# A decoder layer in one kernel: fewer idle products, rotation partners by transfers, and sums, scatters and the last statistics in another order

## The chip, the cores and the metric

The kernel runs on one core of a Trainium2 chip. The metric is the device time of one execution in microseconds (us), the median of several runs. Engines are named as the profile names them: PE is TensorE (PEld its weight loads), DVE is VectorE, ACT is ScalarE, POOL is GpSimd, SP is SyncE, which here only issues transfers.

## The reference, cut to what matters

A decoder layer on `x` of 32 sequences of 128 tokens with 128 features, all float32:

```
x = x + self_attention(layernorm(x))     # 16 heads of 8, rotary positions, softmax over 128 keys
x = x + cross_attention(layernorm(x), ctx)   # ctx: 32 x 77 x 128, softmax over 77 keys
h = layernorm(x)
x = x + layernorm(h + experts(h)) * gamma + beta   # the layernorm of the ffn, eps 1e-5
# experts: logits = h @ Wg + bg, the two largest of 8, softmax over these two;
#          y_e = gelu(h @ W1[e] + b1[e]) @ W2[e] + b2[e]  (128 -> 512 -> 128)
# rotary: q*cos + rot(q)*sin, where rot swaps neighbouring features and negates one of each pair
```

The scatter and gather of the experts' rows is the kernel's own way: the reference computes all eight experts.

## The kernel before

The five engines each have a program of their own, and semaphores tie them. Everything of one core is written out by hand as a list of 64 **steps**. A step is one sequence through one attention. The first 12 steps are self attention alone (sequences 0 to 11), then 20 slots give two steps each, self attention of sequence n and cross attention of sequence n - 12, and the last 12 steps (52 to 63) are cross attention alone. Four sequences make a group; there are eight groups. What is done by group (the normalised and transposed input `xnt`, the projections q, rq, k, rk, v, the same for cross attention, the gate's logits, the places of the routed rows) are **items** that `plan()` (L101) hangs into steps; `jobs` are its other entries for DVE, POOL, ACT and SP.

rq and rk are the rotation's partners: products of the input with weights whose neighbouring columns are swapped. DVE multiplies q by cosines and rq by sines (L1368, from PSUM, with the bias), POOL adds the two (`turned`, L1775), ACT and POOL split the sum into two float16 parts (`high`, `low`), SP parks them in DRAM and spreads them from there over the rows that the scores read.

PE's order in one step (`step`, L984): `shifted(st, 0)` (the transposed scores of heads with the maxima taken off, L841 and L847, and between them the plain scores of the step two ahead, L797), `rows_turned` of the step two back (L891), items, idle products (`dense`, L978), `maxima_turned` (L879), `values` of the step before, second half (L873), items, `projected` (L898, L899), `shifted(st, 1)`, `sums_turned` of the step before (L886, which waits for `s_res`, DVE's residual), items, and `values(st, 0)`, which has idle products of its own in front. The **idle products** multiply constants and write to an unused part of a bank. `idle_at` says how many there are: none in a step with projections, three at each of the two places in other steps, six in the last twelve.

DVE's order: maxima of two banks (L1319), items, `residual` (L1346), maxima of two more, `norm_rows` (L1328, L1330, on the turned sums), `residual_statistics`, items. ACT's: two exponentials (L1140), `rows_out`, `sums_out`, `maxima_out`, items, two exponentials, and `high_part`.

After the gate each token's row goes with an indirect DMA to its two experts' regions in DRAM (`scatter`, L1860), from two to each step. As soon as groups 0 to 5 are there (`EARLY` = 5) and DVE has made the table of the first 40 tiles (`first_owners`, `first_sums`, `first_entries`), the expert stage starts: 71 tiles of 128 rows, each transposed (L1080), multiplied (L1069), passed through gelu (L1269), multiplied (L1095), scaled and scattered (L1931). The last attention step, and the last groups' routing, are folded into its first turns (`between`). At the end both rows of each token are added on PE in eight chunks of four sequences (L1121), DVE takes their statistics, POOL the deviations (L1956 to L1960), ACT normalises (L1289), DVE or POOL multiply by gamma (L528) and DVE adds (L1711).

Of the kernel before, what the change touches and what calls it, by code (L numbers as in the profile page):

```python
# [27 lines left out]
P = 128  # L28
SEQS, L, D, LC = 32, 128, 128, 77
H, HD = 16, 8  # L30
GS = 4
# [39 lines left out]
BETA = 3  # L71
NA = ((EARLY + 1) * TOK * TOPK - E * (P - 1)) // P // ROUND * ROUND
# [28 lines left out]
def plan():  # L101
# [14 lines left out]
    for g in range(NG):  # L116
        own = SELF_STEP[g * GS + GS - 1]
        if g >= 2:
            free = SELF_STEP[(g - 2) * GS + GS - 1]
            made = free if g >= 4 else 3 * g - 4 if g == 3 else 1  # L120
            xnt = made - 1 if g >= 4 else made
            if g == 2:
                job(0, "normed", g)
            else:
                job(xnt - 3, "statistics", g)
                job(xnt - 2, "normed", g)
            put(xnt, 1 if g >= 4 else 0, "xnt", g)
            for k, names in enumerate((("q", "rq"), ("k", "rk"))):
                at, turn = (made, 3) if k and g == 3 else (made + k, 1)
                put(at, turn, names[0], g)  # L130
                put(at, turn, names[1], g)
                job(at, "sum", (g, k))
                job(at + 1, "high", (g, k))
                job(at + 2, "low", (g, k))
                job(at + 2, ("park_q", "park_k")[k], g)
            job(made + 2 if g == 3 else made + 3, "spread", g)
            put(free + 3 if g >= 4 else free + 1, 1, "v", g)
# [68 lines left out]
def decoder_layer(nc, x, ctx_t, w_self, b_self, bp, w_cross, b_cross, bo, wg, bg, w1, b1, w2, b2,  # L206
# [3 lines left out]
    with stack:  # L210
# [230 lines left out]
        s_rhi = sem("s_rhi")  # L441
        s_route = sem("s_route")
# [80 lines left out]
        LAST = CHUNKS - 1  # L523

# [72 lines left out]
        def _(sp):  # L597
# [88 lines left out]
            for n in range(NS):  # L686
# [18 lines left out]
                for g in jobs_at(n, "load_x"):  # L705
                    load_x(g)
                if n == 20:
                    for k in range(2):
                        sp.wait_ge(s_st[k], NJ // 2 * (SELF_STEP[(FAR[-1] + 1) * GS - 1] + 1))
# [62 lines left out]
        def _(pe):  # L772
# [211 lines left out]
            def step(st):  # L984
# [114 lines left out]
            def between(i):  # L1099
                if i == -3:  # L1100
                    sums_turned(STEPS[-1])
# [16 lines left out]
            for n in range(CHUNKS):  # L1118
# [6 lines left out]
        def _(act):  # L1125
# [41 lines left out]
            def work(name, g):  # L1167
                bank, c = item(name, g)
                w = BANKS[bank]
                if name in ("q", "rq", "k", "rk", "log", "pos", "cnt"):  # L1170
                    return
                act.wait_ge(s_w[bank], c)
                if name == "xnt":
# [111 lines left out]
            for i in range(SEQS):  # L1285
                if i % FC == 0:
                    act.wait_ge(s_rsfm, i // FC + 1)
                r = SUM[i // FC][:, (i % FC) * D:(i % FC + 1) * D]
                act.activation(xn3all[:, i * D:(i + 1) * D], r, ACT.Identity,  # L1289
# [3 lines left out]
        def _(dve):  # L1293
# [63 lines left out]
            def work(name, g):  # L1357
# [4 lines left out]

# [185 lines left out]
            def step(st):  # L1548
# [33 lines left out]
                if st.at == COUNTED + 2:  # L1582
                    first_sums()
# [101 lines left out]
            def chunk_statistics(n):  # L1685
                dve.wait_ge(s_add, n + 1)
                for i in range(FC):
                    V.bn_stats(stf[:, n * FC + i, :], SUM[n][:, i * D:(i + 1) * D]).then_inc(s_rawf, 1)
# [3 lines left out]
                dve.wait_ge(s_stf, (n + 1) * FC)  # L1692
                V.tensor_scalar(nmf[:, n * FC:(n + 1) * FC], mvf[:, n * FC:(n + 1) * FC, 0], -1.0, None, ALU.mult).then_inc(s_nmean, 1)
# [33 lines left out]
        def _(pool):  # L1727
# [42 lines left out]
            def turned(g, k):  # L1770

                for name in (("q", "rq"), ("k", "rk"))[k]:
                    bank, c = item(name, g)
                    pool.wait_ge(s_wf[bank], c)
# [89 lines left out]
            def scatters(n, place):  # L1864
                for g, i, k in jobs_at(n, ("scatter", place)):
                    pool.wait_ge(s_st[1], NJ // 2 * n + place + 1)
# [9 lines left out]
            def step(st):  # L1876
# [76 lines left out]
            def inverse_deviations(n):  # L1953
                at = slice(n * FC, (n + 1) * FC)
                pool.wait_ge(s_nmean, n + 1)
                G.tensor_scalar(rsf[:, 1, at], mvf[:, at, 1], 4 * EPS, None, ALU.add).then_inc(s_rsf, 1)  # L1956
                pool.wait_ge(s_rsf, 2 * n + 1)
                G.tensor_tensor(rsf[:, 0, at], rsf[:, 1, at], halff[:, at], ALU.pow).then_inc(s_rsf, 1)
                pool.wait_ge(s_rsf, 2 * n + 2)
                G.tensor_tensor(rsf[:, 1, at], nmf[:, at], rsf[:, 0, at], ALU.mult).then_inc(s_rsfm, 1)  # L1960
# [82 lines left out]
```

## Time and profile before

| | |
|---|---|
| median of 3 runs | 603.55 us (601.19 to 603.73) |
| the profiled execution | 598.75 us, its span 596.9 us |
| busy | PE 519.3, DVE 385.3, POOL 347.1, ACT 324.3 us |
| chain that ended last | PE 57%, issue 11%, DVE 9%, DMA 7%, ACT 6%, SP's queue 5%, POOL 4% |
| granted TensorE clock | 0.978 of full on average |

Busy time is the time in which an engine executed an instruction; the chain is followed back from the last instruction to what released each. The ends of matmuls are modelled, so groups that overlap show more busy time than they take in a row.

### The profile page before, as it was taken

The numbers are of one execution on the slowest core, as the hardware profiler recorded it, in microseconds if no ns is written. First come the engines' busy times: TensorE is split into PE (matmuls) and PEld (weight loads), VectorE is DVE, ScalarE is ACT, GpSimd is POOL, SyncE is SP. The second block draws the span as 40 slices with busy tenths as digits, with TensorE's granted clock in tenths as the row PEclk, the third lists the DMA queues.
The fourth block names the chain that finished last, engine by engine and source line by source line (L and its number), as shares of the span: only waits on it lengthen the run. The fifth ranks groups of instructions, "written<-read, shape, count | busy, mean of one in ns | idle before, by whom it ended". The sixth has DMA issues, their size and how long they took to land.

```text
span 596.9 us, 21959 instructions
## 1 busy us (share of the span) xinstructions
PE 519.3 (87%) x7657; PEld 389.0 (65%) x7658; DVE 385.3 (65%) x1275; ACT 324.3 (54%) x870; POOL 347.1 (58%) x475
## 2 busy tenths in 40 slices
PE   6889998989998998888979998789888899999980
PEld 4456565656655655665657676588877799999530
DVE  5778887777886786685855766544644444445096
ACT  2447565766766666665656465445434455555143
POOL 5748597636438748638573467546554554444374
PEclk8999999999999999999999999889999999999995
DMA  5232340431762403403112210022222222222393
GB/s 155 84 115 71 104 152 28 151 91 52 226 230 87 137 20 87 137 25 102 34 40 74 80 47 25 28 55 60 64 68 80 74 69 57 57 57 59 98 252 88
DMA packets 68785, 52.57 MB, mean 88 GB/s; under 512 B 8752, under 2 KB 65077, under 8 KB 68690
## 3 DMA queue, kind: packets, MB, share of 16 engines
q1 hardware_dynamic: 62994, 41.92, 25.1%
q0 software_dynamic: 4352, 8.53, 4.4%
q8 instruction: 59, 0.97, 0.7%
q10 hardware_dynamic: 1344, 0.85, 0.5%
q14 instruction: 36, 0.29, 0.2%
HBM read 33.10 MB, written 18.64 MB: 87 GB/s over the span
## 4 chain that ended last, share of the span: by engine, by line
PE 57%; issue 11%; DVE 9%; DMA 7%; ACT 6%; SPq 5%; POOL 4%; DVEq 0%; ACTq 0%; POOLq 0%
PE S L1069 8%; PE AV L873 7%; PE AV L1095 4%; PE SM L1095 4%; PE ST L841 4%; PE W L921 4%; PE ST L847 4%; PE SM L886 3%; ACT prob L1140 3%; PE AV L978 3%; PE SM L898 2%; DVE nmp L1319 2%; SPq L637 2%; PE W L934 2%; PE SM L891 2%
## 5 line engine op out<-in xcount | busy, mean ns | idle before, releaser
L1140 ACT ACTIVATE prob<-ST 128x512 f32<-128x512 f32 (+1 forms) x256 | 138.4, 592 | 117.3 <-PE ST L847 111.1
L1319 DVE TENSOR_REDUCE nmp<-S 128x4 bf16<-128x308 f32 (+1 forms) x251 | 134.6, 576 | 15.8 <-PE S L797 10.0
L1269 ACT ACTIVATE va<-S,b1s 128x128 f32<-128x128 f32 x284 | 81.1, 369 | 81.0 <-PE S L1069 66.8
L1931 POOL DMA_INDIRECT expert_out<-va,ks x71 | 70.0, 985 | 73.4 <-DVE va L1644 44.7
L1860 POOL DMA_INDIRECT routed<-pay,dest x64 | 65.9, 1029 | 33.3 <-PE ST L847 20.2
L873 PE MATMUL AV<-prob,va 77*32 77x128 f32 (+1 forms) x2048 | 84.4, 280 | 0.6 <-issue 0.5
L1069 PE MATMUL S<-va 128*128 128x128 f32 x568 | 77.7, 280 | 7.6 <-issue 5.5
L841 PE MATMUL ST<-nmt,onesr 32*77 32x128 bf16 (+1 forms) x1024 | 73.7, 219 | 8.9 <-ACT prob L1140 3.3
L1069 PEld LDWEIGHTS S<-va 128*128 128x128 f32 x568 | 70.3, 195 | 10.1 <-issue 8.8
L841 PEld LDWEIGHTS ST<-nmt,onesr 32*77 32x77 bf16 (+1 forms) x1024 | 52.4, 102 | 33.5 <-issue 31.8
L873 PEld LDWEIGHTS AV<-prob,va 77*32 77x32 f32 (+1 forms) x2048 | 49.0, 109 | 24.4 <-issue 20.8
L1828 POOL TENSOR_SCALAR ve<-mv 128x1 f32<-128x1 f32 x64 | 15.7, 245 | 62.2 <-DVE mv L1355 61.7
L886 PE MATMUL SM<-idf,ots 128*128 128x128 f32 x128 | 27.2, 294 | 16.5 <-DVE x L1346 11.3
L1095 PE MATMUL AV<-w2s,va 128*128 x288 | 40.6, 284 | 0.0
L1830 POOL TENSOR_TENSOR rs<-ve,half 128x1 f32<-128x1 f32 x64 | 36.7, 574 | 5.3
L1095 PE MATMUL SM<-w2s,va 128*128 x280 | 39.4, 284 | 0.0
L1644 DVE SCALAR_TENSOR_TENSOR va<-AV,ks 128x128 f32<-128x128 f32 x36 | 12.6, 351 | 40.3 <-remote 15.0
L978 PE MATMUL AV<-onesr,idb 128*128 128x256 bf16 x255 | 38.0, 273 | 0.3 <-ACT x2all L1134 0.3
L847 PE MATMUL ST<-q2s,k2s 32*77 32x128 f16 x512 | 35.8, 214 | 0.0
L1095 PEld LDWEIGHTS AV<-w2s,va 128*128 128x128 f32 x288 | 35.0, 192 | 0.8
L1631 DVE COPY va<-w1s 128x512 f32 x71 | 30.5, 430 | 6.9 <-PE S L1069 5.3
L1095 PEld LDWEIGHTS SM<-w2s,va 128*128 128x128 f32 x280 | 34.0, 192 | 0.7
(278 smaller groups left out, 1133.2 us busy)
## 6 DMA issues: line engine op xcount, KB each, us to landing
ks<-routed SPq DMA_DIRECT2D x72, 65.0 KB
q2s<-q_parts SPq DMA_DIRECT2D x32, 128.0 KB
qs<-q_parts SPq DMA_DIRECT2D x20, 128.0 KB
ks<-k_parts SPq DMA_DIRECT2D x20, 128.0 KB, 2.7
k2s<-k_parts SPq DMA_DIRECT2D x32, 77.0 KB
xin<-x SPq DMA_DIRECT2D x8, 256.0 KB, 3.4
q_parts<-q2part SPq DMA_DIRECT2D x8, 256.0 KB
w1s<-w SPq DMA_DIRECT2D x8, 256.0 KB, 4.4
```

What stands on the lines that cost most here:

```text
L841: mm(o, onesr[rows, b, 0:st.keys], nmt[rows, st.at % 2, :], start=True, stop=False)
L847: ins = mm(o, k, q, start=False, stop=True)
L873: last = mm(AV[32 * c:32 * c + 32, m * L:(m + 1) * L], v[0:st.keys, st.group % 2, at:at + VW], prob[0:st.keys, j, b * L:(b + 1) * L], star ...
L886: last = tr(TURNED[:, m * L:(m + 1) * L], ots[:, m * L:(m + 1) * L], idf[:, :])
L978: mm(bank, idb[:, :], some[:, 0:bank.shape[1]], start=True, stop=True)
L1069: last = mm(S[k][:, q * P:(q + 1) * P], w1c[:, k, q * P:(q + 1) * P], xt[:, (c + 1) % 4, :], start=True, stop=True)
L1095: last = mm(o, ht[:, (c - 1) % 4, q, :], w2s[:, bass.ds(e * (HID // D) + q * D, D)], start=False, stop=(q == HC - 1))
L1140: act.activation(prob[0:st.keys, j, :], ST[j % 2][0:st.keys, :], ACT.Exp, scale=SCALE).then_inc(s_exp, 1)
L1269: last = act.activation(ht[:, (c + 1) % 4, q, :], S[k][:, q * P:(q + 1) * P], ACT.Gelu, bias=b1s[:, bass.ds(b + q, 1)])
L1319: V.tensor_reduce(nmp[:, st.at % 2, row_tile(p), 0:NB], bank[:, 0:NB * st.keys].rearrange("p (b k) -> p b k", b=NB), AX.X, ALU.max, negate ...
L1860: pool.indirect_dma_start(out=routed, out_offset=bass.IndirectOffsetOnAxis(ap=dest[:, g % 2, i, k:k + 1].bitcast(U32), axis=0), in_=pay[:, ...
L1931: pool.indirect_dma_start(out=expert_out, out_offset=bass.IndirectOffsetOnAxis(ap=xr[:, at % ROUND, D + 1:D + 2].bitcast(U32), axis=0), in ...
```

## The change

- For groups 4 to 7 (`SWAP` = 4) rq and rk are not made. ACT moves q (and k) with its bias from PSUM to `rb`; SP copies the odd partitions of `rb` to the even ones of `ra` and the other way round; one step later DVE multiplies `ra` by sines and `rb` by cosines (`rotate`), and POOL adds. All that follows of these groups comes one step later.
- `idle_at`: the second place has none in steps without projections (3 before), and 3 in the last twelve (6 before). The first place keeps its numbers. The first three turns of the expert stage get two idle products of 512 columns each.
- `sums_turned` stands behind `values(st, 0)` instead of in front of it.
- Group 5's eight scatters are in three steps (3, 3, 2) instead of four; the table of the first tiles is made one step earlier.
- In the last stage the first chunk is summed in two halves in two banks, and the negated means are computed by POOL instead of DVE.

```diff
+SWAP = 4
@@ plan()
-                put(at, turn, names[1], g)
+                if g < SWAP:
+                    put(at, turn, names[1], g)
+                else:
+                    job(at, "swap", (g, k))
+                    at += 1
+                    job(at, "rotate", (g, k))
...
-            job(made + 2 if g == 3 else made + 3, "spread", g)
+            job(made + 2 if g == 3 else made + 3 if g < SWAP else made + 4, "spread", g)
...
-                    job(chosen + 1 + i, ("scatter", k), (g, i, k))
+                    n = TOPK * i + k
+                    if g == EARLY:
+                        job(chosen + 1 + n // 3, ("scatter", n % 3), (g, i, k))
+                    else:
+                        job(chosen + 1 + i, ("scatter", k), (g, i, k))
@@ sync
+            def swap(g, k):
+                bank, c = item(("q", "k")[k], g)
+                sp.wait_ge(s_wf[bank], c)
+                sp.wait_ge(s_parts, 2 * (g - 1) + k + 1)
+                sp.dma_start(ra[0::2, k, :], rb[1::2, k, :]).then_inc(s_swap[k], 16)
+                sp.dma_start(ra[1::2, k, :], rb[0::2, k, :]).then_inc(s_swap[k], 16)
@@ tensor
-                return 3 if st.slot < SEQS else 6
+                return (3, 0)[m] if st.slot < SEQS else (6, 3)[m]
...
+                background(st, 2)
+                values(st, 0)
                 if before:
                     sums_turned(before)
-                background(st, 2)
-                values(st, 0)
...
             def between(i):
+                if i < 0:
+                    dense(2, ST[1][:, :])
...
-            for n in range(CHUNKS):
+            for m in range(2):
+                at = slice(m * FC // 2 * D, (m + 1) * FC // 2 * D)
+                for k in range(TOPK):
+                    pe.wait_ge(s_y2[k][0], 16)
+                    last = mm((SUM[0], SUM[LAST])[m][:, at], idf[:, :], y2[0][:, k, at], start=(k == 0), stop=(k == TOPK - 1))
+                last.then_inc(s_add, 1)
+            for n in range(1, CHUNKS):
+                if n == LAST:
+                    pe.wait_ge(s_norm, FC)
@@ scalar
+                if name in ("q", "k"):
+                    k = ("q", "k").index(name)
+                    act.wait_ge(s_sum, 2 * (g - 1) + k + 1)
+                    act.activation(rb[:, k, :], w[:, :], ACT.Identity, bias=bqk[:, 2 * k:2 * k + 1]).then_inc(s_wf[bank], 1)
@@ vector
+            def rotate(g, k):
+                dve.wait_ge(s_swap[k], 32 * (g - SWAP + 1))
+                for part, table in ((ra, sinb), (rb, cosb)):
+                    p3 = part[:, k, :].rearrange("p (i l) -> p i l", i=GS)
+                    V.tensor_tensor(p3, p3, table[:, :].unsqueeze(1).to_broadcast([P, GS, L]), ALU.mult).then_inc(s_rot, 1)
...
                 if st.at == COUNTED + 2:
-                    first_owners()
-                if st.at == COUNTED + 3:
+                    first_sums()
                     first_entries()
...
+                for g, k in jobs_at(st.at, "rotate"):
+                    rotate(g, k)
...
                     take_tiles()
-                if st.at == COUNTED + 2:
-                    first_sums()
+                    first_owners()
...
-                V.tensor_scalar(nmf[:, n * FC:(n + 1) * FC], mvf[:, n * FC:(n + 1) * FC, 0], -1.0, None, ALU.mult).then_inc(s_nmean, 1)
@@ gpsimd
             def turned(g, k):
+                if g >= SWAP:
+                    pool.wait_ge(s_rot, 2 * (2 * (g - SWAP) + k + 1))
...
+                scatters(n, 2)
...
-                pool.wait_ge(s_nmean, n + 1)
+                pool.wait_ge(s_stf, (n + 1) * FC)
                 G.tensor_scalar(rsf[:, 1, at], mvf[:, at, 1], 4 * EPS, None, ALU.add).then_inc(s_rsf, 1)
+                G.tensor_scalar(nmf[:, at], mvf[:, at, 0], -1.0, None, ALU.mult).then_inc(s_nmean, 1)
```

## Rows read from the trace of the kernel before

**Rows 1.** Part 1 of the page: busy us (share of the span), instructions.

```profile
PE 519.3 (87%) x7657; PEld 389.0 (65%) x7658; DVE 385.3 (65%) x1275; ACT 324.3 (54%) x870; POOL 347.1 (58%) x475
```

**Rows 2.** Windows: length, busy PE, PEld, DVE, ACT, POOL, clock, DMA share, GB/s.

```profile
36.00:317.00 281.00, 250.85 (x4897) 168.70 (x4890) 212.27 (x656) 175.28 (x423) 176.85 (x254) 1.00 0.33 99
317.00:383.00 66.00, 60.05 (x1130) 44.35 (x1128) 43.25 (x191) 37.74 (x92) 36.31 (x57) 1.00 0.16 45
383.00:396.00 13.00, 8.98 (x58) 7.12 (x58) 5.38 (x21) 4.97 (x15) 6.82 (x14) 0.63 0.21 51
```

**Rows 3.** Groups by form: operation, shapes, count | busy us, mean ns | idle before, releasers.

```profile
L1319 DVE TENSOR_REDUCE nmp<-S 128x4 bf16<-128x512 f32 x123 | 79.1, 683 | 4.4 <-PE S L797 3.8
...
L1860 POOL DMA_INDIRECT routed<-pay,dest x64 | 65.9, 1029 | 33.3 <-PE ST L847 20.2 <-issue 12.8 <-DVE va L1644 0.3
...
L978 PE MATMUL AV<-onesr,idb 128*128 128x256 bf16 x255 | 38.0, 273 | 0.3 <-ACT x2all L1134 0.3
...
L886 PE MATMUL SM<-idf,ots 128*128 128x128 f32 x128 | 27.2, 294 | 16.5 <-DVE x L1346 11.3 <-DVE x2all L1346 4.8
...
L1368 DVE SCALAR_TENSOR_TENSOR rb<-W,bqk,sinb 128x512 f32<-128x512 f32 x14 | 10.5, 748 | 1.4 <-PE W L921 0.5
...
L1192 ACT ACTIVATE q2part<-W,bqk 128x512 f16<-128x512 f32 x8 | 5.5, 687 | 4.9 <-PE W L943 4.9
...
L1393 DVE TENSOR_TENSOR ra<-ra,rb 128x512 f32<-128x512 f32 x2 | 1.4, 692 | 0.2
```

**Rows 4.** The chain: start, us, what; first and last of 11 such pieces.

```profile
114.65 0.33 PE AV L978 x3
...
377.05 0.66 PE AV L978 x6
```

**Rows 5.** Timeline of step 27, where k of group 6 is made.

```profile
178.02 1.98 PE L921 MATMUL W<-xnt,wqk 128*128 128x512 f32 x4
...
179.84 0.38 PE L898 MATMUL SM<-wcross,onormt 128*128 128x128 f32 x2
...
180.04 0.75 DVE L1368 SCALAR_TENSOR_TENSOR rb<-W,bqk,sinb 128x512 f32<-128x512 f32 x1
...
180.71 0.28 DVE L1346 TENSOR_TENSOR x2all<-SM,x 128x128 f32<-128x128 f32 x1
...
182.66 0.33 PE L891 MATMUL SM<-idf,onorm 128*128 128x128 f32 x1
```

**Rows 6.** The chain at the change-over to the experts.

```profile
370.99 1.03 POOL pay L1841
...
380.16 3.88 DMA routed<-pay,dest
...
385.21 0.86 DMA ks<-routed
```

**Rows 7.** Timeline of the last stage.

```profile
557.90 7.51 PE L978 MATMUL W<-onesr,idb 128*128 128x512 bf16 x34 [0.45 <-DVE va L1644]
...
569.01 0.24 POOL L1956 TENSOR_SCALAR xnt<-xnt 128x4 f32<-128x4 f32 x1 [9.05 <-DVE xnt L1693]
...
569.12 0.89 DVE L1688 BATCH_NORM_STATS2 xnt<-S 128x6 f32<-128x128 f32 x4 [0.20 <-PE S L1121]
...
574.93 1.17 DVE L1693 TENSOR_SCALAR xnt<-xnt 128x4 f32<-128x4 f32 x1
...
576.19 0.70 POOL L1956 TENSOR_SCALAR xnt<-xnt 128x4 f32<-128x4 f32 x1
```

**Rows 8.** Who waited for ACT's copy of the rows: us in total, times.

```profile
  PEld SM L898: 12.7, 24
```

**Rows 9.** Timeline of PE at the change-over.

```profile
380.77 0.41 PE L886 MATMUL SM<-idf,ots 128*128 128x128 f32 x2 [1.45 <-DVE x2all L1346]
...
387.10 0.45 PE L1080 MATMUL W<-idf,ks 128*128 128x128 f32 x1 [2.16 <-DMA ks<-routed]
```

**Rows 10.** A window around the change-over, columns as in rows 2.

```profile
380.00:395.00 15.00, 10.20 (x83) 7.85 (x84) 7.09 (x30) 4.87 (x15) 7.07 (x13) 0.66 0.21 50
```

More of the change, by code:

```diff
@@ L441, in decoder_layer @@
         s_rhi = sem("s_rhi")
+        s_swap = [sem(f"s_swap{k}") for k in range(2)]
+        s_rot = sem("s_rot")
         s_route = sem("s_route")
@@ L523, in decoder_layer, with summed @@
         LAST = CHUNKS - 1
+        def summed(i):
+            bank = SUM[LAST] if FC // 2 <= i < FC else SUM[i // FC]
+            return bank[:, (i % FC) * D:(i % FC + 1) * D]
         def times_gamma(eng, first, seqs, s):
@@ L706, in _ @@
                     load_x(g)
+                for g, k in jobs_at(n, "swap"):
+                    swap(g, k)
                 if n == 20:
@@ L1169, in work @@
                 w = BANKS[bank]
-                if name in ("q", "rq", "k", "rk", "log", "pos", "cnt"):
+                if name in ("rq", "rk", "log", "pos", "cnt") or name in ("q", "k") and g < SWAP:
                     return
                 act.wait_ge(s_w[bank], c)
-                if name == "xnt":
+                if name in ("q", "k"):
+                    k = ("q", "k").index(name)
+                    act.wait_ge(s_sum, 2 * (g - 1) + k + 1)
+                    act.activation(rb[:, k, :], w[:, :], ACT.Identity, bias=bqk[:, 2 * k:2 * k + 1]).then_inc(s_wf[bank], 1)
+                elif name == "xnt":
                     move(turned_of(g)[:, :], w[:, :], s_wf[bank])
@@ L1287, in _ @@
                     act.wait_ge(s_rsfm, i // FC + 1)
-                r = SUM[i // FC][:, (i % FC) * D:(i % FC + 1) * D]
-                act.activation(xn3all[:, i * D:(i + 1) * D], r, ACT.Identity,
+                act.activation(xn3all[:, i * D:(i + 1) * D], summed(i), ACT.Identity,
                                bias=rsf[:, 1, i:i + 1], scale=rsf[:, 0, i:i + 1]).then_inc(s_norm, 1)
@@ L1361, in work @@
                 if name in ("q", "rq", "k", "rk"):
+                    if g >= SWAP:
+                        return
                     n = ("q", "rq", "k", "rk").index(name)
@@ L1685, in chunk_statistics @@
             def chunk_statistics(n):
-                dve.wait_ge(s_add, n + 1)
-                for i in range(FC):
-                    V.bn_stats(stf[:, n * FC + i, :], SUM[n][:, i * D:(i + 1) * D]).then_inc(s_rawf, 1)
+                for i in range(n * FC, (n + 1) * FC):
+                    dve.wait_ge(s_add, n + 2 if n or i >= FC // 2 else 1)
+                    V.bn_stats(stf[:, i, :], summed(i)).then_inc(s_rawf, 1)
                 dve.wait_ge(s_rawf, (n + 1) * FC)
@@ L1691, in chunk_statistics @@
                     V.bn_aggr(mvf[:, i, :], stf[:, i, :]).then_inc(s_stf, 1)
-                dve.wait_ge(s_stf, (n + 1) * FC)
-                V.tensor_scalar(nmf[:, n * FC:(n + 1) * FC], mvf[:, n * FC:(n + 1) * FC, 0], -1.0, None, ALU.mult).then_inc(s_nmean, 1)
             gammas = 0
@@ L1770, in turned @@
             def turned(g, k):
-                for name in (("q", "rq"), ("k", "rk"))[k]:
-                    bank, c = item(name, g)
-                    pool.wait_ge(s_wf[bank], c)
+                if g >= SWAP:
+                    pool.wait_ge(s_rot, 2 * (2 * (g - SWAP) + k + 1))
+                else:
+                    for name in (("q", "rq"), ("k", "rk"))[k]:
+                        bank, c = item(name, g)
+                        pool.wait_ge(s_wf[bank], c)
                 G.tensor_tensor(ra[:, k, :], ra[:, k, :], rb[:, k, :], ALU.add).then_inc(s_sum, 1)
@@ L1865, in scatters @@
                 for g, i, k in jobs_at(n, ("scatter", place)):
-                    pool.wait_ge(s_st[1], NJ // 2 * n + place + 1)
+                    pool.wait_ge(s_st[1], NJ // 2 * n + min(place, 1) + 1)
                     scatter(g, i, k)
@@ L1959, in inverse_deviations @@
                 pool.wait_ge(s_rsf, 2 * n + 2)
+                pool.wait_ge(s_nmean, n + 1)
                 G.tensor_tensor(rsf[:, 1, at], nmf[:, at], rsf[:, 0, at], ALU.mult).then_inc(s_rsfm, 1)
```

## The prediction

> **What bounds the kernel now.** I read the totals of the engines first [rows 1]: TensorE (PE) is busy for 87% of the span, no other engine above 65%. Then the stages [rows 2]. The attention stage, 36 to 383 us, is 347 us long; PE works in 250.85 + 60.05 = 310.9 us of it and stands for 36.1 us. From 383 to 396 us the kernel changes over to the experts, and PE works 8.98 of 13.00 us at a granted clock of 0.63. Then the experts run, and the last 40 us are the sum of the two experts' rows, the last normalisation and the stores. The third view is the groups of instructions [rows 3]: the reader is to see that in the attention stage the largest single cause of PE's standing is DVE's residual (L1346), for which the two transposes of the sums (L886) wait 16.5 us in all. The fourth is the chain of work that ended last [rows 4]: idle products are part of it, but few of them. The last views are the timelines of one step, of the change-over and of the end.
>
> So PE is the bound of attention, with DVE close behind (212.27 us of 281). That matters, since several of the edits take work from PE and none from DVE.
>
> **Rotation partners by transfers.** Groups 4 to 7 lose the projections rq and rk. In the step that makes k of group 6 the two products, k and rk, begin at 178.02 us and the next product (L898) at 179.84 [rows 5]: 1.82 us, 0.91 for one. Eight go: 7.3 us off PE. DVE loses 16 passes from PSUM of 748 ns (12.0 us) [rows 3] and gets 16 multiplications of two SBUF operands; the nearest row is L1393, 128x512 with both operands in SBUF, 692 ns [rows 3]: 11.1 us. DVE's load thus stays, but its place moves: from before the residual of the same step to the end of the next step, behind which the next step's maxima wait. ACT gets eight 128x512 passes from PSUM with a bias; the row of the same form is L1192, 687 ns [rows 3]: 5.5 us, while PE's next product, the projection L898 and the shifts go on, and ACT idles there anyway (it is busy 54% of the span [rows 1]). SP issues 16 transfers of 128 KB. What queues behind them on SP are the parks and spreads of the same and the next step. The transfers have a whole step (5.5 us on average: 347 over 63) before DVE asks for them, and a 65 KB load of rows in this trace is there 0.86 us after its issue [rows 6]. I cost them at nothing; if that cover is gone, DVE stands, and behind it all maxima. POOL's sum and the parts come one step later; group 4's rows are then spread three steps before their first use, about 16 us.
>
> How much of 7.3 us stays? In the step of [rows 5] DVE's residual came at 180.71, 0.87 us after the L898 of 179.84, because DVE had the rb pass (0.75 us from 180.04) in front of it; without that, PE is through this step some 0.9 us earlier. But the moved 1.4 us (two of 692 ns) then stand in front of the maxima of the next step, which in that trace have no slack of this size: a DVE pass of 683 ns per bank [rows 3], two banks before the scores can go on. I walked the pair of steps through: PE comes to the transpose L891 of the step after at nearly the same time as before. Bounds: 0 and 7.3 us gained. I take the middle, 3.5.
>
> The Trainium skill, "SBUF — State Buffer", section "Who interferes with whom", says that a VectorE instruction with two SBUF inputs contends with a GpSimd instruction that reads SBUF, and that the second one to issue blocks. This speaks against the change, whose 16 new multiplications are of this kind where the old ones had one operand in PSUM. The end of the kernel shows it: POOL's 128x4 addition takes 0.24 us in the open and 0.70 us beside a DVE pass of two SBUF operands [rows 7]. If each of the 16 held POOL for its whole 0.69 us, it would be 11 us of POOL, which has some 40% free in this stage; the sum stays as it is.
>
> **Fewer idle products.** With no projection in a step there are three idle products (six in the last twelve) at each of two places. The change takes those of the second call (ahead of the transpose of the maxima, L879) away, and three of six in the last twelve: 20 x 3 + 9 x 3 = 87 products. Three take 0.33 us on the chain, six 0.66 [rows 4]: 87 are 9.6 us of PE. The cover of most of them: the projection L898 behind them waits for ACT's copy of the rows, which comes after two exponentials, and would wait longer without them (PE's weight loads waited for this copy in 24 cases even so, 12.7 us in all) [rows 8]. On the chain I count 11 pieces at this place, from 114.65 to 377.05 us, six of 0.33 and five of 0.66 us; what goes is 6 x 0.33 + 5 x 0.33 = 3.6 us. In steps 60 and 61 POOL sets the pace: the transposes L947 wait for its L1841, which ends at 372.02 [rows 6], and POOL's third scatter in step 60 (about 1.0 us [rows 3]) uses what slack it had. I take 0.6 off: 3.0 us. Bounds 0 and 9.6.
>
> **Sums behind values.** The transposes L886 wait for DVE's residual, 16.5 us in total [rows 3]. Behind `values` (L873, 0.57 us) and its idle products that wait is mostly over. But where does the stall go? In the steps in which the residual is late, DVE is late as a whole: after it come two maxima (up to 1.37 us) and only then the two operations on the turned sums, whose result the transpose L891 waits for. In [rows 5]: residual at 180.71, L891 at 182.66, 1.95 us on, and DVE's two maxima and two operations on the sums take most of it. PE arrives earlier at L891 and stands there instead. Only where the two maxima are short (the 308 columns of a cross step, not 512) does something stay. Where the residual was not late, the sums come 0.6 to 0.9 us later to DVE; there DVE is still in its maxima for most of that, so little is lost. I take 4.0 us gained, bounds 3 lost (0.05 in each of 62 steps) and 16.5 gained.
>
> **Scatters and tables one step earlier.** Group 5's last scatter is issued at 380.16 and lands 3.88 us later, SP's first load of rows comes at 385.21 [rows 6], and PE's first transpose of an expert tile waits 2.16 us until 387.10 [rows 9]. Before that PE stood 1.45 us for a residual that DVE reached late, since the table's entries stood in front of it [rows 9]. The granted clock is 1.00 in the whole stage before [rows 2] and 0.66 on average from 380 to 395 us [rows 10]: with TensorE's two levels, 2.4 and 1.2 GHz, that is 0.34/0.5 of 15 us, 10.2 us, at the lower one, just after the pause for the residual. PE was busy for 10.20 of those 15 us, so for about 6.9 at the lower level, half of it lost: 3.5 us. With eight scatters in three steps the last is issued in step 62, near 374.5 instead of 380.16; the table is done in the same step. The data is then there before PE asks. 2.16 + 1.45 + 3.5 = 7.1 us; the six new idle products of 512 columns cost 0.22 each (7.51 us for 34 [rows 7]), 1.3 us: 5.8 us. Bounds: 0.9 (the data wait alone, less the idle products) and 7.1.
>
> **The end.** The first chunk is summed in two banks by halves, so DVE can start half of four passes (1.8 us) earlier, 0.9 us. It gains nothing: DVE comes to the second chunk at 569.12 after a wait for its sum [rows 7] and will wait for it again. The negative mean moves from DVE (L1693; one of the eight took 1.17 us [rows 7]) to POOL, whose addition at 576.19 starts when DVE's mean is there and is followed by powers and the second gamma pass, for which DVE waits. Chunks 1 to 4 lie ahead of that gamma pass, 0.24 us more each: about 1.0 lost; DVE's shorter end and the earlier start of the last deviations give back 0.4. I take 0.6 lost, bounds 1.5 lost and 1.0 gained.
>
> **Sum.** 3.5 + 3.0 + 4.0 + 5.8 - 0.6 = 15.7 us. The profiled execution took 598.75 us (its span of 596.9 and 1.85 around it); it would take 583.1. The runs shown lie higher (601.19 to 603.73); their median of 603.55 less the same sum is 587.9, rounded to 588.
>
> **Rivals.** (1) DVE, not PE, is what attention has to wait for. For it: the step of [rows 5], and that DVE's work is unchanged. Against: DVE is busy 76% there and PE 89%. Then edits one and three give nothing, and the idle products 2 us: 2 + 5.8 - 0.6 = 7.2 us, 596.4. Chance 0.21. (2) PE alone is the bound, and what DVE does fits in beside it: 7.3 + 6 of the idle products + 12 of the 16.5 + 7.1 - 0.6 = 32 us, 571.5. Chance 0.10. (3) The other side: with 87 fewer products PE's clock falls in attention. The mechanism is that of [rows 10]: a pause, and 10.2 us at the lower level. If PE is busy throughout, one such period costs 5.1 us. Four of them (20.4 us) eat the 15.7 us and put it 4.7 us above before, 608; three (15.3) leave it where it was. For it: PE stands for 36.1 us in attention. Against: none of them brought the clock down between 36 and 380 us (1.00 in both stages of [rows 2]), and the change shortens the pauses as well. Chance 0.07. The Trainium skill, "TensorE: Matmul & The Clock Gate", section "HAM oscillation — how this bites in real kernels", describes such a kernel, which loses its clock again and again behind its waits for data; the trace shows this only at the change-over. (4) The swaps come late behind other transfers and DVE stands 1 to 2 us in each of eight steps: 3.5 turns into -8; the sum is 4.2 us, 599. Chance 0.04.
>
> **From this to the numbers.** My forecast (578 to 595) has 0.58, the four rivals 0.42. Half a per cent, 3 us, is about what can be told from no change here: faster means under 600.5. That holds for the forecast, for rival 2, and for nearly all of rival 1; rival 4 lies near the edge. Faster 0.84, same 0.08, slower 0.08. The range that leaves no more than two in ten outside reaches down to near rival 2 and up over rival 1: 575 to 600.
>
> **What the profile after would show.** L978 on AV 168 times instead of 255; L921 16 instances fewer. PE's wait in front of L886 nearly gone, and a wait in front of L891 on DVE's onorm, some microseconds. DVE's rotations at about 690 ns without a wait for a transfer. The attention stage 10 us shorter. SP's first load of rows right behind step 62 and no PE wait of 2 us behind the last L899; a clock at 1.00 through the change-over. At the end L1693 gone and POOL's part of the chain longer, the last stage no shorter. What would make me wrong: a granted clock below 1.00 inside attention; a gain in attention over 20 us (DVE has more slack than I give it), or under 4 (it has none); the clock still falling at the change-over.

## The result, and the profile after

The changed kernel takes 623.01 us (median of 4 runs, 621.33 to 625.55) against 603.64 us before: 1.033 of the time of before, 95% interval 1.028 to 1.038. It is slower, where I had forecast 588 us. Here and below, medians are over all runs, while ratios and intervals leave out the runs that lie more than 1.5% above the fastest of the same kernel, so a ratio need not be the quotient of two medians.

Part 1 and the clock line of the page of the changed kernel (the second is in 40 slices of the span, in tenths of full speed):

```profile
PE 538.8 (87%) x7564; PEld 397.3 (64%) x7565; DVE 380.8 (61%) x1267; ACT 329.9 (53%) x878; POOL 348.1 (56%) x483
...
PEclk9999798996999898998959886699899999999995
```

Its windows, with the columns of [rows 2]; the third is the place of [rows 10]:

```profile
36.00:317.00 281.00, 251.72 (x4645) 165.93 (x4645) 205.31 (x638) 174.88 (x415) 170.93 (x246) 0.92 0.34 103
317.00:383.00 66.00, 58.48 (x1025) 40.89 (x1019) 36.80 (x149) 33.51 (x83) 30.52 (x51) 0.86 0.19 53
383.00:396.00 13.00, 12.71 (x133) 8.38 (x133) 7.81 (x29) 5.68 (x14) 8.86 (x11) 0.50 0.07 23
```

The clock was 1.00 in the first two of these windows before [rows 2]; now it is 0.92 and 0.86. The trace has eleven periods at the lower level between 36 and 400 us where before had one, at the change-over. The last exponential of attention starts at 402.7 us, not at 379.9: all of the loss is there.

Groups of the changed kernel, with the columns of [rows 3]:

```profile
L1007 PE MATMUL AV<-onesr,idb 128*128 128x256 bf16 x168 | 29.3, 304 | 1.5 <-ACT nmt L1174 1.1 <-ACT x2all L1174 0.3
L915 PE MATMUL SM<-idf,ots 128*128 128x128 f32 x128 | 29.2, 312 | 1.7 <-DVE x L1389 1.4
L920 PE MATMUL SM<-idf,onorm 128*128 128x128 f32 x64 | 22.0, 343 | 5.2 <-DVE onorm L1373 1.6 <-issue 1.4
L950 PE MATMUL W<-xnt,wqk 128*128 128x512 f32 x32 | 17.4, 648 | 1.5 <-ACT xnt L1174 1.5
L1371 DVE RECIPROCAL rden<-SM 128x16 f32<-128x16 f32 x64 | 16.2, 253 | 36.7 <-PE SM L915 35.2 <-issue 1.5
L1437 DVE TENSOR_TENSOR rb<-rb,cosb 128x512 f32<-128x512 f32 x8 | 5.5, 683 | 0.0
L1437 DVE TENSOR_TENSOR ra<-ra,sinb 128x512 f32<-128x512 f32 x8 | 5.3, 661 | 0.0
```

The mechanics are as forecast: 168 idle products, 16 instances fewer of the projection, rotations of 0.66 to 0.68 us without a wait for a transfer, PE's wait ahead of the sums (now L915) down from 16.5 to 1.7 us, and a wait of 5.2 us ahead of the next transpose (L920). One row was not forecast: DVE stands 36.7 us in front of its reciprocal (L1371), waiting for the turned sums. The same row before:

```profile
L1328 DVE RECIPROCAL rden<-SM 128x16 f32<-128x16 f32 x64 | 15.8, 248 | 1.9 <-PE SM L886 1.9
```

The reader is to see in the longer means of PE's rows (304 ns for an idle product, 273 before [rows 3]) that the clock is mixed into every duration.

### The profile page after: what moved, and what is told of

Its sections match the earlier page's. It is cut to its first block, busy times and chain, and to the rows that moved or that the text cites. A ratio compares the mean times of both kernels' runs of the same rounds, so it can differ in the third digit from the quotient of the medians.

```text
span 619.5 us, 21797 instructions
## 1 busy us (share of the span) xinstructions
PE 538.8 (87%) x7564; PEld 397.3 (64%) x7565; DVE 380.8 (61%) x1267; ACT 329.9 (53%) x878; POOL 348.1 (56%) x483
## 4 chain that ended last, share of the span: by engine, by line
PE 55%; DVE 12%; issue 9%; DMA 6%; POOL 6%; ACT 5%; SPq 5%; another core or an unknown queue 1%; DVEq 1%; POOLq 0%; ACTq 0%
PE S L1098 8%; PE AV L902 7%; PE AV L1124 4%; PE ST L870 4%; ACT prob L1180 4%; PE SM L1124 4%; DVE nmp L1362 4%; PE ST L876 4%; PE W L950 3%; PE AV L1007 3%; PE SM L927 3%; SPq L656 2%; PE S L826 2%; PE SM L915 2%; PE SM L920 2%
## 5 line engine op out<-in xcount | busy, mean ns | idle before, releaser
L870 PE MATMUL ST<-nmt,onesr 32*77 32x128 bf16 (+1 forms) x1024 | 82.9, 231 | 17.9 <-ACT prob L1180 10.6
L902 PE MATMUL AV<-prob,va 77*32 77x128 f32 (+1 forms) x2048 | 89.8, 295 | 0.3 <-issue 0.3
L870 PEld LDWEIGHTS ST<-nmt,onesr 32*77 32x77 bf16 (+1 forms) x1024 | 56.8, 109 | 43.9 <-issue 42.3
L902 PEld LDWEIGHTS AV<-prob,va 77*32 77x32 f32 (+1 forms) x2048 | 51.7, 115 | 24.0 <-issue 17.8
L876 PE MATMUL ST<-q2s,k2s 32*77 32x128 f16 x512 | 40.8, 230 | 0.0
L1371 DVE RECIPROCAL rden<-SM 128x16 f32<-128x16 f32 x64 | 16.2, 253 | 36.7 <-PE SM L915 35.2
L826 PE MATMUL S<-k2s,q2s 32*128 32x77 f16 x512 | 32.0, 209 | 1.4 <-DVE nmp L1362 1.4
```

The costliest lines, as they stand in the source:

```text
L826: ins = mm(scored(st, p)[:, b * st.keys:(b + 1) * st.keys], q, k, start=True, stop=True)
L870: mm(o, onesr[rows, b, 0:st.keys], nmt[rows, st.at % 2, :], start=True, stop=False)
L876: ins = mm(o, k, q, start=False, stop=True)
L902: last = mm(AV[32 * c:32 * c + 32, m * L:(m + 1) * L], v[0:st.keys, st.group % 2, at:at + VW], prob[0:st.keys, j, b * L:(b + 1) * L], star ...
```

## The experiments

The experiments ran in five groups (e1 to e4, e5 to e8, e9 to e12, e13 to e16, e17 and e18), each on a chip of its own, and each is compared with before on the same chip. Before takes 604.9 us (median) on the first chip and 579 to 583 on the other four.

**Which edit brings the clock down?** Four kernels. The changed kernel with `idle_at` of before (e1), with the sums turned where they were (e2); the kernel before with the one (e3) or the other (e4) edit alone.

```diff
# e1 (on the changed kernel); e3 is the same edit the other way round, on the kernel before
-                return (3, 0)[m] if st.slot < SEQS else (6, 3)[m]
+                return 3 if st.slot < SEQS else 6
# e2 (on the changed kernel); e4 the other way round, on the kernel before
+                if before:
+                    sums_turned(before)
                 background(st, 2)
                 values(st, 0)
-                if before:
-                    sums_turned(before)
```

> The changed kernel with the idle products of before (three at both places, six at both in the last twelve steps). Theory A, the 87 missing idle products let the granted clock fall twelve times in attention: the clock is at 1.00 in attention again, and the time falls below before, to 585 to 595 us, since the other edits then give what they give. Theory B, the other order of sums and values opens the clock's way: the periods at the lower clock stay, at least half of them, and the time stays above 612. Theory C, the lower clock is a companion and VectorE's new wait for the turned sums costs the time: the clock returns but the time stays above 605.

> The changed kernel with the sums turned ahead of the values, as before. Theory A (idle products): the clock still falls about as often, 615 us or more. Theory B (order of sums): the clock stays up, below 600 us. Theory C (VectorE waits for the sums): VectorE's 35 us of waiting in front of the reciprocal go, and the time falls below 605 whatever the clock does.

> The kernel before with only the number of idle products changed. Theory A: the clock falls in attention, 612 to 625 us. Theory B: the clock stays at 1.00 until the change-over, 598 to 602 us (3 us of idle products gained). Neither: the clock falls only with both, and this run is as before within 3 us.

> The kernel before with only the sums behind the values. Theory A: the clock stays up, 598 to 603 us (my term of 4 us, or less). Theory B: the clock falls in attention, 612 us or more. Theory C: the clock stays up and the kernel is slower than 606 us.

Measured, against 604.93 of before: e1 621.98 us, ratio 1.028 (1.016 to 1.039); e2 612.67, 1.016 (1.002 to 1.030); e3 608.95, 1.013 (1.003 to 1.022); e4 632.06, 1.036 (1.021 to 1.051). Theory A falls with e1 (clock 0.929 to 0.946 although the products are back), theory B alone with e2 and e3. Either edit alone brings the clock down on this chip: mean clocks of 0.970 for before, 0.953 for e3 and 0.926 for e4. Windows of e4:

```profile
36.00:317.00 281.00, 255.16 (x4703) 168.04 (x4703) 205.99 (x637) 170.59 (x407) 169.48 (x244) 0.96 0.32 96
317.00:383.00 66.00, 61.73 (x954) 43.38 (x955) 33.14 (x129) 32.72 (x79) 27.63 (x43) 0.76 0.19 51
```

**What is left, and the other parts alone.** e8 is the changed kernel with both put back; e5 is before with the swaps alone, e6 with the scatters, the table and the six idle products, e7 with the new end.

```diff
# e8 (on the changed kernel): both edits of e1 and e2
# e5, e6, e7 (on the kernel before): of the change's diff only SWAP, swap() and rotate(); only scatter, tables and dense(2, ST[1]); only the last stage
```

> The changed kernel with both the order of the sums and the idle products of before: what is left is swaps, scatters and tables, and the end. Theory D, order and idle products between them cause all of the falls of the clock: 590 to 597 us, the clock 0.97 or more over the span. Theory E, the swaps (eight float32 products fewer on PE) bring the clock down too: above 600 us with the clock under 0.965.

> The kernel before with only the rotation partners by transfers. Theory D: 597 to 603 us, the clock as before; my term of 3.5 us gained, within 0 and 7. Theory E: the clock falls between 100 and 280 us, where groups 4 to 7 are made, and the run is 3 us or more slower than before.

> The kernel before with only the scatters three a step, the table one step earlier and the six idle products in the first expert turns. My term of 5.8 us gained: 596 to 601 us, no PE wait of 2 us for the first tile, and no period at the lower clock at the change-over. Rival: the clock falls there all the same, and at most 3 us are gained.

> The kernel before with only the new last stage. My term: 0.6 us slower, within 1.0 gained and 1.5 lost, which the time can't show; the distance from PE's first sum to the last instruction in the profile does, 31.5 us before, 31 to 33 here. Rival: VectorE's lighter chain gives 2 us or more, and the distance is under 30.

Measured, against 581.08 of before: e8 578.91 us, ratio 0.997 (0.992 to 1.002); e5 576.39, 0.996 (0.991 to 1.001); e6 583.40, 1.014 (1.002 to 1.027); e7 583.00, 1.012 (0.999 to 1.025). In e7 the first sum of the last stage starts at 550.8 of a span of 582.0: 31.2 us, 31.5 before (565.4 of 596.9). With both edits put back the loss is gone: e8 can't be told from before (the changed kernel itself did not run on this chip; it lost 1.8 and 3.3% where it ran). But its mean clock, 0.959, is still under before's 0.968, so neither theory D (0.97 or more) nor theory E (a time well above before) holds as it was written. The scatters alone gain nothing, where 5.8 us were forecast; whether they lose can't be told, since e7, whose edit touches only the last stage, measures the same. The timeline of PE and POOL in e6 shows where the gain may have gone:

```profile
357.21 1.07 POOL L1865 DMA_INDIRECT routed<-pay,dest  x1 [0.18 <-PE ST L852]
358.58 0.99 POOL L1865 DMA_INDIRECT routed<-pay,dest  x1 [0.30 <-issue]
359.88 1.18 POOL L1865 DMA_INDIRECT routed<-pay,dest  x1 [0.30 <-issue]
...
362.10 0.81 POOL L1846 TENSOR_SCALAR pay<-x2all,mv,rs 128x128 f32<-128x128 f32 x1
...
363.05 0.63 PE L952 MATMUL W<-idf,pay 128*128 128x128 f32 x4 [2.41 <-POOL pay L1846]
```

Three scatters in a row stand in front of the normalisation that PE's transposes of group 6 wait for. PE stands 2.41 us, and the clock is at 0.50 from 365 us on for 17 us. That is one trace; e9 tests it.

**Scatters as 2, 3, 3, and the order of the sums in part.** e9 is e6 with the eight scatters as 2, 3, 3, so that the third comes one step later, behind the normalisation; e12 is e8 with the same. e10 turns the sums behind the idle products but ahead of the values; e11 has the full order in steps 0 to 51 alone.

```diff
# e9 (on e6) and e12 (on e8)
-                        job(chosen + 1 + n // 3, ("scatter", n % 3), (g, i, k))
+                        job(chosen + 1 + (n + 1) // 3, ("scatter", n if n < 2 else (n + 1) % 3), (g, i, k))
# e10 (on before)
                     dense(idle_at(st, 0), AV[:, 2 * L:4 * L])
+                    if turn:
+                        sums_turned(turn)
...
-                if before:
-                    sums_turned(before)
                 background(st, 2)
-                values(st, 0)
+                values(st, 0, before)
# e11 (on before)
+                late = st.slot < SEQS
-                if before:
+                if before and not late:
                     sums_turned(before)
                 background(st, 2)
                 values(st, 0)
+                if before and late:
+                    sums_turned(before)
```

> The kernel before with the scatters of group 5 as 2, 3, 3 in steps 60 to 62 (not 3, 3, 2), the table one step earlier and the six idle products. Theory F: in the 3, 3, 2 order the third scatter stood on GpSimd ahead of the normalisation for which PE's transposes in step 62 wait, 2.41 us there, and the clock fell 2 us behind that pause. Then here that wait is 1.0 us or less, the clock stays up at the change-over or falls late, and 3 to 6 us are gained on before. Rival: the gain of the earlier data is lost at the change-over whatever the order, and the run is within 2 us of before.

> The kernel before with the sums turned behind the idle products but ahead of the values, so that the wait for the residual is covered by 0.33 us (0.66 in the last twelve steps) and VectorE gets the sums 0.57 us sooner than in the full edit. Theory G, what costs in the full edit is VectorE's wait for the sums: that wait is under 10 us here (18 to 35 us in the full edit, 2 before) and the time is within 2 us of before, the clock as before. Rival H, any sums behind the idle products bring the clock down: 6 us or more slower, with the clock below 0.96.

> The kernel before with the sums behind the values in steps 0 to 51 alone; the last twelve keep the order of before. If the long period at the lower clock (70 us in one run of the full edit) comes from the last twelve steps, this run has less than half of the full edit's loss: 8 us or less slower than before. If the loss is spread over all steps, it is 18 us or more slower.

> The changed kernel with sums and idle products as before and the scatters as 2, 3, 3. If the parts add up (swaps 5 us, scatters 3 to 6 us, end nothing): 8 to 11 us faster than before. If the swaps' lighter PE lets the clock fall more often, as in the run with 3, 3, 2: 2 us faster or less.

Measured, against 579.14: e9 574.82 us, ratio 0.990 (0.985 to 0.994); e10 585.75, 1.006 (1.001 to 1.010); e11 581.16, 1.004 (1.000 to 1.007); e12 571.55, 0.982 (0.974 to 0.991). In e9 the same transposes wait 1.06 us and the first tile 0.95, and the clock is whole from 317 to 396 us:

```profile
365.89 0.63 PE L952 MATMUL W<-idf,pay 128*128 128x128 f32 x4 [1.06 <-POOL pay L1846]
...
377.16 0.30 PE L1085 MATMUL W<-idf,ks 128*128 128x128 f32 x1 [0.95 <-DMA ks<-routed]
```

e12 beats before by its interval; the changed kernel, which did not run beside it, loses to before wherever it ran. e12 is 7.6 us faster where 8 to 11 were expected. In e9 the wait and the clock at the change-over came out as theory F said (1.06 us for "1.0 or less"). In e10 theory G fails by its own terms and rival H comes nearer: DVE's wait is 11.8 us and not under 10, the median is 6.6 us over before, and the mean clock is 0.956 against 0.970:

```profile
L1328 DVE RECIPROCAL rden<-SM 128x16 f32<-128x16 f32 x64 | 16.0, 249 | 11.8 <-PE SM L888 10.7 <-issue 0.5
```

**Where, and can more idle products help?** e13 is the changed kernel once more; e14 has the order of the sums in the last twelve steps alone, e15 the same with ten idle products at the first place there; e16 is e12 with the second place empty in steps 2 to 51.

```diff
# e14 (on before): as e11, with
+                late = st.slot >= SEQS
# e15 (on e14)
-                return 3 if st.slot < SEQS else 6
+                return 3 if st.slot < SEQS else (10, 6)[m]
# e16 (on e12)
-                return 3 if st.slot < SEQS else 6
+                return (3, 0)[m] if st.slot < SEQS else 6
```

> The changed kernel as it is, beside before on the chip of this call: 16 to 24 us slower than before if the loss is the kernel's and not the first chip's; the clock between 0.91 and 0.94.

> The kernel before with the sums behind the values in the last twelve steps alone. The same edit in steps 0 to 51 cost 2 us. If the last twelve steps are where the order brings the clock down: 10 to 20 us slower, with the lower clock for 40 us or more between 320 and 400 us. If it takes both parts together: under 5 us slower.

> As the run with the sums behind the values in the last twelve steps, and ten idle products instead of six in front of those values. If PE's lack of work there brings the clock down, more idle products bring it back: the lower clock in those steps is less than half as long, and the run is faster than the one without them although it has 36 products (4 us) more. If it is the order as such, the clock falls as long and the run is up to 4 us slower.

> The fastest combination so far (swaps, scatters as 2, 3, 3, the new end; 1.8% faster than before) with the idle products of the second place gone in steps 2 to 51 but all six kept in the last twelve. If what the idle products cost in the run with them alone was the clock in the last twelve steps: 1 to 3 us faster than that combination, 2.0 to 2.4% faster than before. If the clock falls between steps 2 and 51 as well: less than 1.5% faster than before.

Measured, against 582.53: e13 595.87 us, ratio 1.018 (1.006 to 1.030); e14 580.61, 1.001 (0.996 to 1.005); e15 589.50, 1.016 (1.007 to 1.025); e16 571.99, 0.985 (0.976 to 0.994). The loss of the changed kernel is there on this chip too, smaller: 13 us where 16 to 24 were expected, at a mean clock of 0.935. On this chip the order of the sums in the last twelve steps costs nothing that can be told (e14), and it cost 2 us in the others on the third chip (e11). That doesn't clear either part, since the full order did not run alone on these two chips, and on the fifth it leaves the clock alone too (e17). Whether more idle products bring a lost clock back stays untested: e14 had lost none (mean clock 0.976, 0.969 for before). The four more in each of nine steps cost e15 9 us at the same clock (0.975), more than their own 4; why is open. e16, with 60 of the 87 idle products gone, is 1.5% under before, which can't be told from the 1.8% of e12.

**The two edits once more on another chip.** e17 is e4 again, e18 is e3 again.

> The kernel before with the sums behind the values in all steps, once more, on a chip of this call. If both parts of it together (steps 0 to 51 cost 0.4%, the last twelve nothing) make no more than their sum: 0 to 5 us slower than before, and the 27 us of the first call were that chip's. If the full edit falls over an edge that neither part reaches: 10 us or more slower, the clock 0.02 or more under before's.

> The kernel before with only the number of idle products changed, once more. On the first chip it was 4 us slower with the clock 0.007 under before's. If this holds here: 2 to 7 us slower. If the fewer products are worth what the chain said and the clock is not touched on this chip: 1 to 4 us faster.

Measured, against 581.29: e17 582.68 us, ratio 1.004 (1.001 to 1.008); e18 589.11, 1.011 (1.006 to 1.015), 7.8 us slower where 2 to 7 were expected. On this chip the order of the sums leaves the clock alone and the fewer idle products bring it down. DVE's wait for the sums in e17 is long all the same, 24.5 us where before had 1.9:

```profile
L1328 DVE RECIPROCAL rden<-SM 128x16 f32<-128x16 f32 x64 | 16.2, 253 | 24.5 <-PE SM L886 24.1
```

Windows of e18, which has the lower clock in both parts of attention:

```profile
36.00:317.00 281.00, 255.35 (x4898) 171.47 (x4899) 213.85 (x663) 176.04 (x427) 177.96 (x257) 0.96 0.34 100
317.00:383.00 66.00, 60.87 (x1035) 44.39 (x1033) 41.34 (x186) 35.62 (x86) 35.02 (x57) 0.85 0.15 41
```

**All chips together.** Every run lists its span and mean granted clock. With two levels the time at the lower one is 2 x (1 - clock) x span. I fitted the times of all 200 runs on the five chips, those of before too, by one constant for each kernel and chip and one slope for that time. The slope is 0.365 us of device time for each microsecond at the lower level; what remains is 1.9 us (root mean square). This splits each difference to before in two: what the edit does at the same clock, and what it does by the clock.

| edit on before | at equal clock | by the clock | forecast |
|---|---|---|---|
| swaps (e5) | -5.1 | -0.9 | -3.5 |
| fewer idle products (e3, e18) | -3.0, -2.0 | +7.6, +9.1 | -3.0 |
| sums behind values (e4, e17) | +6.0, +5.7 | +20.8, -3.3 | -4.0 |
| scatters and table (e6) | -0.3 | +1.7 | -5.8 |
| the same as 2, 3, 3 (e9) | -1.4 | -4.9 | |
| end (e7) | -0.3 | +1.7 | +0.6 |
| the whole change (e13) | -1.0 | +15.3 | -15.7 |
| e12 | -5.4 | -3.6 | |
| both put back (e8) | -4.9 | +3.8 | |
| sums between idle products and values (e10) | -0.5 | +6.4 | |
| sums behind values, steps 0 to 51 (e11) | +2.6 | -1.0 | |
| the same, last twelve steps (e14) | +1.8 | -2.9 | |

All in us; a kernel with four runs is good to some 2 us in either column. The five parts at equal clock sum to about -2.3 (the idle products and the sums by their means), the whole to -1.0: they add up. It is a fit, and the clock of a run is no cause that I set; but kernels that differ in nothing but the chance of the run lie near the same line (before's own runs on one chip: 574.6 us at a clock of 0.98 and 597.0 at 0.936; a fit to before's 81 runs alone gives 0.38). The split leans on the longest runs: without the 38 that the ratios leave out the slope is 0.31, and the column at equal clock moves by up to 3.7 us (e4 +9.7, e18 -0.3, e5 -4.2, e13 +2.6). That the swaps gain, that the order of the sums loses and that the whole gains nothing that can be told stands either way.

## Why the prediction was wrong

**The step that failed** is that the sum has no term for the clock in attention: the clock was taken to stay at 1.00 there, and the case that it falls was left to rival 3, "with 87 fewer products PE's clock falls in attention", at a chance of 0.07. The runs showed 0.92 and 0.86 in the two windows of attention in its place. My reason was that none of PE's pauses brought the clock down between 36 and 380 us in the one trace that I had. That trace was of a kernel at the edge: the runs of before have clocks from 0.936 to 0.981, and e6, e7 and e9, whose steps are those of before up to 350 us, have one, three and two periods at the lower level between 36 and 320 us. Of e7:

```profile
36.00:317.00 281.00, 255.93 (x4972) 173.99 (x4976) 214.77 (x665) 179.39 (x427) 177.60 (x256) 0.98 0.34 101
```

The price of a microsecond at the lower level was fair: 0.5 us if PE is always busy, and the fit says 0.365. The changed kernel's trace has 78 us there ahead of the last stage, that of before 14; 64 x 0.365 = 23 us, and the two profiled executions are 22.6 us apart. Rival 3 had reckoned with four such periods beside a gain of 15.7 us; there were eleven.

**And the gain was not there.** At equal clock the five parts sum to -2.3 us by the fit where I forecast -15.7, so most of the gain was missing even apart from the clock. Two terms make the difference: the sums behind the values (9.8 us) and the scatters (5.5 us).

Some of the falls come just behind a long pause. Rows of PE and windows around them in the changed kernel:

```profile
66.13 0.23 PE L870 MATMUL ST<-nmt,onesr 32*128 32x128 bf16 x2 [2.05 <-DMA w1s<-k_parts]
...
95.13 0.23 PE L870 MATMUL ST<-nmt,onesr 32*128 32x128 bf16 x2 [1.75 <-DMA q2s<-q_parts]
...
307.66 0.49 PE L927 MATMUL SM<-wcross,onormt 128*128 128x128 f32 x2 [1.76 <-ACT onormt L1174]
...
376.94 0.17 PE L986 MATMUL W<-seenb,onesb 128*128 128x8 bf16 x1 [1.24 <-POOL seenb L1905]
```

```profile
62.00:66.00 4.00, 2.08 (x6) 0.77 (x6) 2.94 (x8) 0.54 (x2) 1.59 (x2) 1.00 0.70 211
67.00:73.00 6.00, 6.00 (x81) 3.57 (x81) 2.73 (x6) 3.93 (x9) 1.29 (x3) 0.50 0.01 3
93.00:97.00 4.00, 2.25 (x50) 1.58 (x49) 1.90 (x7) 1.34 (x5) 2.23 (x4) 1.00 0.33 99
98.00:100.00 2.00, 2.00 (x25) 1.18 (x24) 0.29 (x1) 0.69 (x1) 1.20 (x1) 0.50 0.00 0
306.00:308.00 2.00, 0.34 (x3) 0.32 (x3) 0.48 (x1) 1.63 (x5) 1.62 (x4) 1.00 0.12 35
310.00:322.00 12.00, 12.00 (x151) 7.30 (x143) 4.67 (x15) 5.35 (x14) 7.22 (x10) 0.50 0.06 18
378.00:396.00 18.00, 17.71 (x205) 11.65 (x199) 9.90 (x36) 6.85 (x16) 11.49 (x14) 0.50 0.08 25
```

The four rows end pauses of 1.2 to 2.1 us, and the clock is down within 2 us behind each. Others of the eleven periods have no such pause ahead of them (those from 144.8, 168.7 and 213 us); the changed kernel also had pauses of 1.37 us (to 193.65) and 1.15 us (to 248.11) without a fall, and before of 1.43 us (to 92.00) and six of about 1.0. So the length of a pause alone does not settle it. Why the sums behind the values bring the clock down on one chip, by 57 us in the mean, and not on another is open: PE's standing in attention is no longer (26.8 us between 38 and 340 us in e4, 30.4 before), and neither the last twelve steps nor the others alone did it on the chips where they ran. That either edit alone can bring the clock down is shown (e3, e4, e18), and that without both the loss is gone and most of the clock is back (e8, 0.959 against 0.968 for before); by what path the order does it is not. What I cited beside rival 3 from the Trainium skill, "TensorE: Matmul & The Clock Gate", section "HAM oscillation — how this bites in real kernels", a kernel that loses its clock again and again behind its waits for data, pointed the right way: the changed kernel's trace agrees for the falls behind the waits of 2.05 and 1.75 us for transfers, not for the three without such a pause. My remark that the trace shows this only at the change-over held for that one trace.

**Rotation partners: right, and under-sized.** 5.1 us gained for 3.5, within the bounds. I had halved the 7.3 us because the rotations stand in front of DVE's maxima; the run keeps more. The transfers hid, as costed (2.1 us from issue to landing in the median, and no rotation waits for one), and ACT's passes did. Of the holding of POOL by the new multiplications little can be seen, since nine of the sixteen have no POOL instruction beside them; the two scatters that ran beside two rotations each (at 194.22 and 237.83 us) took 1.35 and 1.24 us where the mean is 1.04.

**Idle products: right in size at equal clock,** 2.0 to 3.0 us for 3.0 (0.3 to 2.3 without the longest runs). The term left out the clock, which cost 7.6 and 9.1 us.

**Sums behind values: wrong in sign, at equal clock too.** I wrote that DVE is still in its maxima when the sums come and that little is lost. The row of the reciprocal refutes it, 24.5 to 42.7 us of standing in front of it where before had 1.9: DVE, which I had called close to PE as a bound, was made to wait in each step for what it had at once before. Of PE's 16.5 us ahead of the sums nearly all went, as forecast, and came back elsewhere; the net is 5.8 us lost. My bound of 3 us lost was too narrow. e10, which gives DVE the sums 0.57 us sooner (11.8 us of standing), loses nothing at equal clock (-0.5); its clock was lower all the same (6.4 us by it). e14 and e11, with 12.2 and 14.2 us of standing, lose 1.8 and 2.6, e17 and e4, with 24.5 and 42.7, 5.7 and 6.0. That fits the wait as the price, though no run sets the wait alone.

**Scatters and table: 5.8 us forecast, 0.3 found.** The data is early, as forecast: between the last exponential and the first tile lie 3.6 us (402.7 to 406.3) where before had 7.2. I saw that POOL sets the pace in steps 60 and 61 and took 0.6 us off; in e6 it was a pause of 2.41 us for PE, and the fall of the clock, whose absence was to give 3.5 us of my 5.8, came earlier and lasted longer (17 us for 10.2). With the third scatter one step later (e9) the run is 4.3 us faster than before, 1.4 at equal clock and 4.9 by the clock in the fit.

**The end: nothing,** 0.3 us for my 0.6 the other way, both under what can be told.

## What to carry to other kernels

A mean granted clock of 0.98 in one trace doesn't say that the kernel keeps its clock: look at the clock of every run, and if it scatters (0.936 to 0.981 over 81 runs here), take each product away from PE, idle ones too, as a risk with a price, and split what you measure by the clock of the runs before you judge an edit. A wait that is taken from one engine by moving its work back is paid by whoever reads the result: look at what the reader did at that time, not only at what the waiting engine did. A list of edits should be run one by one: of five here, only the swaps came out ahead in time (0.996, at the edge of what can be told), and the whole loses; the swaps, the new end and the scatters as 2, 3, 3 together are 1.8% faster than before (0.9 to 2.6%).

## What the runs showed that I had not expected

The same kernel takes 604.9 us on the first chip and 579 to 583 on four others, at the same mean clock (0.968 to 0.970 on all five). A good part of the difference lies with the experts: from the first tile's transpose to the first sum of the last stage it is 179.9 us in e3 on the first chip (390.5 to 570.4), 167.8 in e7 (383.0 to 550.8) and 168.9 in e17 (380.5 to 549.4) on two others, with the same instructions there. And the same edit, the order of the sums, brings the mean clock down by 0.044 on the one (e4) and not at all on another (e17, 0.976 against 0.968 for before).
